# Normalised x kept in DRAM from phase 4 to phase 6, instead of computed twice, in a recurrent block with a gated MLP

## What is computed

```python
xn = _layernorm(x, axis=-1)
s = _L0_attn_ref(xn, ...)      # complex recurrence over time with 256 states, y = C_re H_re - C_im H_im + D * xn
g = _silu(_L0_ffn_ref(xn, ...))
x = x + s * g

def _L0_ffn_ref(x, ...):
    routed = sigmoid(x @ w_router + b_router) > 0.5
    h1 = rmsnorm(x, norm1_w)
    h = x + (h1 @ wv + bv) @ wo
    h2 = rmsnorm(h, norm2_w)
    processed = h + (silu(h2 @ w_gate) * (h2 @ w_up)) @ w_down
    return where(routed, processed, x)
```

## Time and profile before

| what | value |
|---|---|
| median of 2 runs | 3838.17 us (3834.44 to 3841.89) |
| the profiled execution | 3831.34 us, span 3829.5 us |
| spans of the 8 cores | 3801.1 to 3829.5 us |
| PE (TensorE matmuls) busy | 2676.6 us (70%) |
| DVE (VectorE) busy | 1116.6 us (29%) |
| ACT busy | 413.8 us (11%) |
| moved by DMA | 354.71 MB |

### The profile page before, as it was taken

How to read it: one execution, slowest core, us unless ns; L and a number is a source line. 1 busy time by engine, 2 the same in 40 slices (tenths; PEclk the granted TensorE clock), 3 DMA queues, 4 the chain that set the end, 5 groups by cost and what they waited for, 6 DMA issues and landing times.

```text
span 3829.5 us, 31001 instructions; the slowest of 8 cores (3801.1 to 3829.5 us)
## 1 busy us (share of the span) xinstructions
PE 2676.6 (70%) x11744; PEld 1144.4 (30%) x11744; DVE 1116.6 (29%) x1265; ACT 413.8 (11%) x491; POOL 363.7 (9%) x311
## 2 busy tenths in 40 slices
PE   6230425389399999966667637884999999567665
PEld 1010102133144444422223213331444444223222
DVE  1556475624401001122322241252111101232233
ACT  2130000211200000000000012112000000000000
POOL 0000000011011111100000001110111111000000
PEclk9675768699699999988888868997999999788888
DMA  6050524569677777755654555777777776654564
GB/s 185 14 187 25 150 73 151 115 68 131 146 74 77 76 76 76 75 72 89 95 78 84 90 114 72 94 110 137 77 77 77 77 76 69 99 81 81 91 95 69
DMA packets 723123, 354.71 MB, mean 93 GB/s; under 512 B 681994, under 2 KB 684058, under 8 KB 718237
## 3 DMA queue, kind: packets, MB, share of 16 engines
q0 software_dynamic: 679728, 178.28, 47.0%
q1 hardware_dynamic: 43250, 174.46, 13.8%
HBM read 497.34 MB, written 33.61 MB: 139 GB/s over the span
## 4 chain that ended last, share of the span: by engine, by line
PE 60%; DMA 19%; DVE 12%; issue 3%; ACT 2%; POOL 1%; PEld 1%; DVEq 1%; PEldq 1%; ACTq 0%; SPq 0%; POOLq 0%
PE ps L154 60%; DMA arena<-down_p 10%; DVE arena L158 5%; DMA arena<-xNB 3%; ACT arena L175 2%; DMA arena<-xT 2%; DVE arena L178 2%; POOL arena L148 1%; DMA arena<-up_p 1%; DVE arena L162 1%; DMA arena<-wv_p 1%; PEld ps L154 1%; DVE arena L170 1%; DMA arena<-wo_p 1%; DMA hspill<-arena 1%
## 5 line engine op out<-in xcount | busy, mean ns | idle before, releaser
L154 PE MATMUL ps<-arena 128*128 128x512 bf16 x11264 | 2543.2, 388 | 840.9 <-DMA arena<-down_p 412.7
L154 PEld LDWEIGHTS ps<-arena 128*128 128x128 bf16 x11264 | 1112.4, 100 | 2270.2 <-issue 1020.8
L158 DVE TENSOR_TENSOR arena<-arena,ps 128x512 bf16<-128x512 f32 (+1 forms) x240 | 165.0, 687 | 1257.5 <-ACT arena L175 1121.3
L158 DVE TENSOR_TENSOR arena<-arena,m_bc 128x1024 f32<-128x1024 f32 x96 | 117.6, 1225 | 1026.7 <-ACT arena L175 812.4
L175 ACT ACTIVATE arena<-ps 128x512 f32<-128x512 f32 x240 | 143.3, 597 | 1981.8 <-PE ps L154 1959.5
L158 DVE TENSOR_TENSOR arena<-arena 128x1024 f32<-128x1024 f32 (+8 forms) x195 | 216.5, 1110 | 44.4 <-DMA hspill<-arena 16.3
L175 ACT ACTIVATE arena<-arena 128x2048 bf16<-128x2048 bf16 (+4 forms) x103 | 140.4, 1363 | 715.3 <-DVE arena L158 237.0
L148 POOL DMA_DIRECT2D arena<-gate_p x88 | 100.6, 1143 | 1128.3 <-PE ps L154 993.2
L148 POOL DMA_DIRECT2D arena<-down_p x64 | 86.0, 1350 | 987.1 <-PE ps L154 987.1
L154 PE MATMUL ps<-arena,ones_bf 128*1 128x512 bf16 x256 | 70.7, 400 | 138.0 <-DVE arena L178 119.8
L178 DVE CAST arena<-arena 128x1024 bf16<-128x1024 f32 (+1 forms) x96 | 83.7, 872 | 214.5 <-PE ps L154 83.5
(11 more groups left out here) (49 smaller groups left out, 379.2 us busy)
## 6 DMA issues: line engine op xcount, KB each, us to landing
arena<-xT SPq DMA_DIRECT2D x128, 512.0 KB, 4.9
arena<-gate_p POOLq DMA_DIRECT2D x88, 512.0 KB, 6.3
arena<-up_p POOLq DMA_DIRECT2D x88, 512.0 KB, 8.1
arena<-down_p POOLq DMA_DIRECT2D x64, 704.0 KB, 10.2
arena<-xT SPq DMA_DIRECT2D x16, 1024.0 KB, 6.4
arena<-xNB SPq DMA_DIRECT2D x16, 1024.0 KB, 10.4
arena<-xNB SPq DMA_DIRECT2D x32, 512.0 KB, 5.7
arena<-wv_p POOLq DMA_DIRECT2D x32, 512.0 KB, 6.3
```

The costliest lines, as they stand in the source:

```text
L154: E.matmul(o, l, r, start=a, stop=b), inc=inc)
L158: E.tensor_tensor(o, a, b, al), inc=inc)
```

## The change

Phase 4 computes xn into a buffer of its own, x4tmp (kilobytes 136 to 140), stores it to a new DRAM tensor xnspill, and adds it to the banks into h_pl[d]. There is one such buffer: the next block's subtraction waits until the store has landed (sO). To make room, hsq4 becomes one buffer, and the statistics matmuls run one block behind instead of two. The h2 loop, which uses the same kilobytes, waits for the last store. In phase 6 the subtraction and the multiplication are gone; SP loads xn from xnspill into t6a, between the loads of h and of x, and VectorE waits for it (sH[1]). In the first block of a half SP waits for the H operations before this load, as their scratch lies in the same place.

```diff
@@ in build_nc
+    xnsp = nc.dram_tensor("xnspill", [D, T], F32)
...
-    hsq4 = [arB(140, TS), arB(138, TS)]
+    x4tmp = arF(136, TS)
+    hsq4 = arB(140, TS)
@@ phase4, for d in range(NK)
             wait("vector", sX[0], mk_x)
-            mk_xc[d] = tt("vector", h_pl[d], xb4, m_bc[:, c0:c0 + TS],
+            wait("vector", sO, sO.v)
+            mk_xc[d] = tt("vector", x4tmp, xb4, m_bc[:, c0:c0 + TS],
                           AL.subtract, inc=sV)
-            tt("vector", h_pl[d], h_pl[d], r_bc[:, c0:c0 + TS], AL.mult)
+            mk_xn = tt("vector", x4tmp, x4tmp, r_bc[:, c0:c0 + TS], AL.mult,
+                       inc=sV)
+            wait("sync", sV, mk_xn)
+            dma("sync", sO, xnsp[d * 128:(d + 1) * 128, c0:c0 + TS], x4tmp)
             wait("vector", sT, mk_grp[d])
...
-                                      h_pl[d][:, q * 512:(q + 1) * 512],
+                                      x4tmp[:, q * 512:(q + 1) * 512],
                                       ps[bank][:, :], AL.add, inc=sV)
-            if d >= 2:
-                dd = d - 2
+            if d >= 1:
+                dd = d - 1
                 wait("tensor", sS, mk_sq[dd])
...
-            if d >= 2:
-                wait("scalar", sT, mk_stq[d - 2])
-            mk_sq[d] = act(hsq4[d % 2], h_pl[d], AF.Square, inc=sS)
+            if d >= 1:
+                wait("scalar", sT, mk_stq[d - 1])
+            mk_sq[d] = act(hsq4, h_pl[d], AF.Square, inc=sS)
...
-        h2tmp = [xb4, arF(136, TS)]
+        h2tmp = [xb4, x4tmp]
+        wait("vector", sO, sO.v)
@@ phase6, for d in range(NK)
             mk_h = dma("sync", sH[0], p6h,
                        hsp[d * 128:(d + 1) * 128, c0:c0 + TS])
+            if d == 0:
+                wait("sync", sV, mk_Hc)
+            mk_xn2 = dma("sync", sH[1], t6a,
+                         xnsp[d * 128:(d + 1) * 128, c0:c0 + TS])
             if d >= 1:
                 wait("sync", sOut[(d - 1) % 2], out_done[d - 1])
...
-            tt("vector", t6a, p6x, m_bc[:, cc:cc + TS], AL.subtract)
-            tt("vector", t6a, t6a, r_bc[:, cc:cc + TS], AL.mult)
+            wait("vector", sH[1], mk_xn2)
             tt("vector", t6b, t6b, p6h, AL.add)
```

More of the change, by code:

```diff
@@ L709, in phase4 @@
                     mk_stq[dd] = mm(ps[4 + q][0:1, :], ones_bf[:, :],
-                                    hsq4[dd % 2][:, q * 512:(q + 1) * 512],
+                                    hsq4[:, q * 512:(q + 1) * 512],
                                     dd == 0, dd == NK - 1,
@@ L713, in phase4 @@
             wait("scalar", sV, mk_hq[2 * d + 1])
-            if d >= 2:
-                wait("scalar", sT, mk_stq[d - 2])
-            mk_sq[d] = act(hsq4[d % 2], h_pl[d], AF.Square, inc=sS)
+            if d >= 1:
+                wait("scalar", sT, mk_stq[d - 1])
+            mk_sq[d] = act(hsq4, h_pl[d], AF.Square, inc=sS)
             if d == NK - 1:
[L718 to L724, removed]
+                wait("tensor", sS, mk_sq[d])
+                for q in range(2):
+                    mk_stq[d] = mm(ps[4 + q][0:1, :], ones_bf[:, :],
+                                   hsq4[:, q * 512:(q + 1) * 512],
+                                   d == 0, d == NK - 1,
+                                   inc=sT if q == 1 else None)
         wait("vector", sT, mk_stq[NK - 1])
```

## The result

The changed kernel takes 3917.4 us in the median of all its executions; against the kernel before the ratio is 1.0185, 95% interval 1.0133 to 1.0237. The change makes the kernel slower by 51 to 91 us; the forecast was 3843 us with a range to 3885. The profiled execution took 3908.6 us, on core 0 as the slowest.

What follows compares the result with a forecast made beforehand. The prediction took TensorE, idling for weights, as the bound. Tails -5.2, phase 6 collisions +6 and phase 4 weights +4 made +5 us on the median 3838.2, so 3843 us, range 3827 to 3885.

Steps and rivals of the forecast that it cites:

- The bounds: Whole kernel: TensorE bound, idling for weights, mostly down_p in phase 6; phase 4 has TensorE busy 88 of 90 us.
- the tails: Phase 6, last block of each half: two VectorE operations less on the exposed path, 2 x 2.60 = -5.2 us.
- +0.2 us in each of 30 blocks: Phase 6: earlier store and loads run into the tail of the down_p weight load, +6 us in all.
- The sum of +1: Phase 6 in all: -5.2 us for the exposed tails and +6 us for transfers colliding with weight loads.
- rival A: Phase 6's two exposed tails are all, transfers hit weight queues without effect: -5 us, 3833 us; chance 25%.
- Rival B: DMA engines full: phase 4 block needs 8.5 us, +27 us; phase 6 even split, +25; 3885 us; chance 16%.
- the price on the weights: Phase 4: the added store delays wo_p to 6.9 us, still covered; 0.15 us in 28 blocks, +4 us.
- the loop: Phase 4, subtraction to next subtraction through store and x load: P = 3.06 + L, costed at 0, upper bound 26 us.
- B's sign: Phase 4: a block of 8.3 us or more with TensorE waiting for wo_p.
- C's: Phase 4: TensorE waiting for ACT's square or VectorE's additions, subtractions more than 8.3 us apart.
- Rival C: Phase 4: slow store through one buffer stops VectorE, P 11.8, +104 us, 3943 us; decides from L of 5.3; chance 5%.
- The sum: Whole kernel: -5.2 + 6 + 4 = +5 us, forecast 3843 us, chance 54%.

Runs made afterwards that it cites:

- e2: Kernel before with only the change's phase 6, its added load reading x in place of x_n; runs 3836.4 and 3833.6 us, no ratio.
- e6: e4 with a 512 KB read of x, used by nobody, in place of the store; 1.0085 to the kernel before.
- e4: Changed kernel with phase 6 as before, x_n stored from four buffers, next x load issued ahead of the store; 1.0075 to the kernel before.
- e14: e12 with two x buffers and x loaded two blocks ahead; 1.0056 to the kernel before.
- e7: e4 with only the first 512 of 1024 columns of each block stored; 1.0034 to the kernel before.
- e12: e4 with the change's order on SP's queue, the store ahead of the next x load; 1.0189 to the kernel before.
- e9: Kernel before with both column groups run on down_p's first half, then both on its second; 0.9001 to the kernel before.
- e11: e9 with the block's result written to t6a and stored from there, SP's wait for the store moved to VectorE; 0.9145 to the kernel before.

## Why the prediction was wrong, point by point

- **The bounds, right.** Phase 6 waits for down_p, VectorE is beside the path in 30 of 32 blocks, phase 4 leaves its DMA engines little room. (The block from 974.51 to 982.03 takes 7.52 us, not 7.54; nothing hangs on it.)
- **Phase 6, right in its parts; the sum can't be told.** Forecast -5.2 for the tails and +0.2 us in each of 30 blocks. TensorE's waits for down_p grew by 0.23 to 0.26 us a block (e2, changed). The sum of +1 stands against -1.2 and -2.7 in the stage table, whose scatter of 7 us would hide rival A's -5 as well. Rival B's +20 (25 less the 5 of the tails) is out.
- **Phase 4, the price on the weights: the size was off.** The step that failed: "A whole 512 KB load beside it thus costs a weight load 0.3 us", so 6.9 us "still covered", and +4 us. A second transfer made wo_p land 1.3 to 1.6 us later (e6, e4), not 0.3, and 22 to 30 us were lost (e14, e4). The comparison of wo_p with wv_p was of a first transfer beside the weights; it says nothing of a second. Rival B's 27 us, from the queues' packet times, was right in size for phase 4; e7, whose two measures disagree on half the bytes, leaves open whether the price goes with the packets' time. The argument by which I cut it down, that two weight loads follow each other at 2.9 us in phase 5, is about one queue, not two. Its price for phase 6, 25 us, was not borne out.
- By rival B's even sharing SP's transfer costs the weight load the transfer's own time. Phase 4 agrees: wo_p lands 1.3 to 1.6 us later for a transfer of 1.5 us of packets. Phase 6 does not: 0.25 us for up to 1.64 us of overlap is well under an even split. The Trainium skill (page "DMA: Bandwidth & Descriptors", section "Queues, rings and completion order") says that each DMA engine takes turns between the queues that have work for it, a packet at a time. Phase 4 agrees with that rule; phase 6 shows that less than an even share can be lost.
- **Phase 4, the loop: the formula held, the step behind it fell.** The period is P = 3.06 + L, with L the landing of x. In the second half on core 0 the chain of waits runs through thirteen landings of x, 7.0 us in the mean in the changed kernel (4.9 to 12.0) and 6.3 in e12, so P is 10.1 and 9.4; the last twelve steps between subtractions measure 10.2 and 9.5. What failed is the step that put the loop at 0: "Between these the loop settles: the later its transfers slip, the more they fall into the gap". They did not: the subtractions came 10.7 us apart, over the limit of 8.33, in the mean over both halves and all cores. My reading is that once VectorE sets the pace, TensorE, and with it the issue of wo_p, follows VectorE, so the transfers keep meeting; the stretch at 909.39 to 924.33 above shows one such meeting. The upper bound given, 26 us, took L at 6.1 and was also too small: the coupling costs 37 us (e12 less e4) to 45 (e12 less e14).
- **The signs.** B's sign came (TensorE waits for wo_p) and C's came too (TensorE waits for ACT's square, subtractions over 8.3 us apart). Rival C, at 5%, named this loop and its deciding point, L over 5.3, but tied it to slow stores through one buffer; the culprit was x behind the store on SP's queue (e12: four buffers, nearly the same loss). By its formula the measured L of 7.0 gives 15 x (10.1 - 8.33) x 2 = 53 us, and its own 104 us was too much.
- **The sum.** 22 to 30 us of traffic and 40 to 48 of loop and buffer make up the 70 us (e14 and e4 against the changed kernel). The two were rivals in the text, and both came true at once. The range ended at the one.

## What to carry to other kernels

When a transfer is added, don't price it by the landing times of transfers that already fit: count the packet time of all queues against the period, and where the sum is over it (8.5 against 7.5 us here), take the excess as the forecast, not as a rival. Then write down every loop buffer, issue, landing, operation with the landing as it will be under the new load; don't count on a loop that sets the pace to slip into a gap by itself. And the place of a load on its queue counts as a dependence: here a store ahead of the next load, not its bytes, was over half of the loss, and issuing the load first or one block earlier removes that part. None of this makes the change pay: the work that it takes from VectorE fell into VectorE's idle time. What did pay was to free a weight buffer half a block earlier (e9), twice over: TensorE waits less, and its granted clock reads 1.00 where it was 0.83.

## What the runs showed of the hardware that was not expected

- The DMA share is no measure of room left. Before, phase 4 reads 0.92 with 136 GB/s; e4 (core 3) reads 1.08 with 182 GB/s over the same 90 us, so the packets' times overlap, and 0.92 did not mean that 8% were left. More was moved, and yet wo_p landed 1.6 us later.

```profile
890.00:980.00 90.00, 82.57 (x364) 33.84 (x362) 38.91 (x41) 10.57 (x10) 11.67 (x11) 0.98 1.08 182
```

- A read and a write of 512 KB beside a casting weight load cost phase 4 the same within the scatter (+27.6 and +30.2 us).
- Taking a wait off SP's queue made phase 6 42 us longer (e11 against e9).
- A long wait of TensorE costs more than its own length. In phase 6 of the changed kernel TensorE starts a block after a wait of 11.2 us (11.60 before), and the matmuls behind it at first start 0.43 us apart (the clock's lower level, 1.2 GHz), then 0.21 (the upper, 2.4 GHz). The weight loads into the array, one for each matmul, show the step on core 0 (start, length, and in brackets the idle time before each):

```profile
2266.42 0.15 PEld L155 LDWEIGHTS ps<-arena 128*128 128x128 bf16 x1 [0.28 <-issue]
2266.85 0.15 PEld L155 LDWEIGHTS ps<-arena 128*128 128x128 bf16 x1 [0.27 <-issue]
...
2267.22 18.44 PEld L155 LDWEIGHTS ps<-arena 128*128 128x128 bf16 x86 [0.21 <-issue]
```

  With the waits cut to about 1 us a block (e9) the granted clock is 1.00 and a block's 96 matmuls take 20.88 us, not 22.75.
